# AdaLN feed-forward kernel on Trainium2: GpSimd issues three of the opening loads, and SP and ScalarE issue fourteen of the first block's sixteen squares

## The reference

```python
w = weights[conditions]                               # 128 of 200 matrices, 32x32
hidden = einsum('bct,bcd->bdt', x, w)                 # (128, 32, 256)
h = square(relu(hidden @ up_w))                       # 256 -> 1024
shared = h @ down_w                                   # 1024 -> 256
scale = top_k(hidden @ gate_w, 2)[0].sum(-1)          # 8 experts
y = shared + (hidden @ expert_weight) * scale
out = x + layernorm(y) * gamma + beta
```

## Time and profile before

| | us |
|---|---|
| median of 3 runs (229.6 to 229.78) | 229.66 |
| the profiled execution, whole | 229.29 |
| its span, first to last instruction | 227.6 |
| PE busy in the span | 220.9 |
| DVE (VectorE) busy | 160.9 |
| POOL (GpSimd) busy | 131.4 |
| ACT (ScalarE) busy | 106.4 |

### The profile page before, as it was taken

One profiled execution on the slowest core, in us unless ns is written; L12 is line 12 of the kernel. 1 busy time (PEld: TensorE's weight loads), 2 busy tenths in 40 slices (PEclk: granted clock), 3 DMA queues, 4 the chain that ended last, 5 costly groups with the idle time before them and its releaser, 6 DMA issues.

```text
span 227.6 us, 3998 instructions
## 1 busy us (share of the span) xinstructions
PE 220.9 (97%) x1260; PEld 191.4 (84%) x1260; DVE 160.9 (71%) x352; ACT 106.4 (47%) x187; POOL 131.4 (58%) x131
## 2 busy tenths in 40 slices
PE   7899999999999999999999999999999999999992
PEld 2798888888888889888889888888888888888892
DVE  6587965777667777667667766577766766777885
ACT  3379865444555345534545444544454444444000
POOL 3758795665545763656455764366555575557411
PEclk9999999999999999999999999999999999999999
DMA  3877123030603010000200002000020002000031
GB/s 98 231 213 230 50 59 103 10 98 7 187 10 98 9 66 30 0 0 3 92 0 0 3 0 95 3 0 0 0 95 1 0 0 68 28 0 0 10 108 69
DMA packets 17177, 11.81 MB, mean 52 GB/s; under 512 B 6660, under 2 KB 16900, under 8 KB 17156
## 3 DMA queue, kind: packets, MB, share of 16 engines
q1 hardware_dynamic: 15460, 10.43, 15.1%
q10 hardware_dynamic: 1280, 1.07, 1.4%
q0 software_dynamic: 416, 0.05, 0.2%
HBM read 7.35 MB, written 4.19 MB: 51 GB/s over the span
## 4 chain that ended last, share of the span: by engine, by line
PE 94%; DMA 1%; issue 1%; DVE 1%; ACTq 1%; POOLq 0%; POOL 0%; ACT 0%; DVEq 0%
PE up_ps L337 39%; PE down_ps L431 25%; PE down_ps L433 13%; PE hid_ps L303 5%; PE moe_ps L449 3%; PE moe_ps L448 3%; PE moe_ps L447 3%; DMA wd<-in_L_cond_weights_dram 1%; PE down_ps L303 1%; ACTq L513 1%; DMA cond_row<-in_itok_B_dram 1%; POOLq L46 0%; POOL rstd L697 0%; DVE result L615 0%; DVE stats L588 0%
## 5 line engine op out<-in xcount | busy, mean ns | idle before, releaser
L682 POOL TENSOR_TENSOR sq_lo<-square,sq_hi 128x512 fp32r<-128x512 f32 x64 | 84.4, 1322 | 77.0 <-DVE square L553 77.0
L431 PE MATMUL down_ps<-down_hl,sq_hi 128*128 128x512 f32 x248 | 88.8, 393 | 0.0
L553 DVE SCALAR_TENSOR_TENSOR square<-up_ps,relu 128x512 f32<-128x512 f32 x64 | 44.0, 687 | 37.3 <-ACT relu L491 28.2
L433 PE MATMUL down_ps<-down_hl,sq_lo 128*128 128x256 f32 x248 | 69.6, 280 | 0.0
L431 PEld LDWEIGHTS down_ps<-down_hl,sq_hi 128*128 128x128 f32 x248 | 46.5, 188 | 10.8 <-issue 0.3
L491 ACT ACTIVATE relu<-up_ps 128x512 f32<-128x512 f32 x64 | 38.2, 596 | 35.8 <-PE up_ps L337 35.7
L337 PE MATMUL up_ps<-hid_hi,up_hi 128*128 128x512 f32 (+1 forms) x136 | 52.8, 391 | 0.3 <-ACT hid_hi L476 0.3
L337 PE MATMUL up_ps<-hid_hi,up_lo 128*128 128x512 f32 (+1 forms) x136 | 51.1, 379 | 0.0
L433 PEld LDWEIGHTS down_ps<-down_hl,sq_lo 128*128 128x128 f32 x248 | 46.7, 188 | 2.4
L493 ACT ACTIVATE sq_hi<-relu 128x512 fp32r<-128x512 f32 x64 | 40.6, 634 | 2.0
L337 PE MATMUL up_ps<-hid_lo,up_hi 128*128 128x512 f32 (+1 forms) x136 | 40.6, 381 | 0.0
(11 more groups left out here) (62 smaller groups left out, 193.3 us busy)
## 6 DMA issues: line engine op xcount, KB each, us to landing
x_sb<-in_x_dram SPq DMA_DIRECT2D x7, 512.0 KB, 4.2
out_dram<-result SPq DMA_DIRECT2D x7, 512.0 KB, 3.0
wd<-in_L_cond_weights_dram SPq DMA_DIRECT2D x111, 4.0 KB, 1.5
x_sb<-in_L_ffn_down_w_dram SPq DMA_DIRECT2D x2, 512.0 KB, 4.7
x_sb<-in_x_dram ACTq DMA_DIRECT2D x2, 256.0 KB, 2.9
result<-in_L_ffn_up_w_dram ACTq DMA_DIRECT2D x2, 256.0 KB, 2.9
result<-in_L_ffn_up_w_dram SPq DMA_DIRECT2D x1, 512.0 KB, 4.7
out_dram<-result SPq DMA_DIRECT2D x4, 128.0 KB, 1.7
```

The costliest lines, as they stand in the source:

```text
L431: pe.matmul(dst[:, :], a_hi, down_hl[:, c, :, :].rearrange("p s t -> p (s t)"), start=(c == 0), stop=False)
L433: mm = pe.matmul(dst[:, T:2 * T], a_lo, down_hl[:, c, 0, :], start=False, stop=(c == CH - 1))
L553: dve.scalar_tensor_tensor(square[:, c % 2, :], up_ps[c % UPB][:, :], 0.0, relu[:, c % 2, :], ALU.max, ALU.mult).then_inc(square_done, 1)
L682: pool.tensor_tensor(sq_lo[:, j % 2, c, :], square[:, c % 2, :], sq_hi[:, j % 2, c, :].bitcast(f32), ALU.subtract).then_inc(sq_lo_done, 1)
```

## The change

GpSimd's list begins with three bulk loads: up's second quarter, x's second half and up's second half, ahead of its registers and squares. ScalarE's and SP's loads of these are gone. Of block 0's squares SP issues 0, 1, 4, 5 and 12 to 15, ScalarE 2, 3, 6, 7 and 8, 9 (all before `split_up(0)`), GpSimd 10 and 11, after a new wait for x's first half. Of block 1's squares SP issues six and GpSimd ten. There is now one semaphore for each group's squares and one for GpSimd's two; PE waits for group 2 and group 3 apart. VectorE rounds and splits up's second half in two parts, one before the first square, the other around the second one. Bytes and arithmetic are the same.

```diff
-UP_SPLITS = [slice(0, 2), slice(2, 4), slice(4, CH)]
+UP_LOADS = [slice(0, 2), slice(2, 4), slice(4, CH)]
+UP_SPLITS = [slice(0, 2), slice(2, 4), slice(4, 6), slice(6, CH)]
-BY_SP, BY_ACT, BY_POOL, BY_SP_LATER = (0, 2, 4, 6), (1, 3, 5, 7), (8, 9, 10, 11, 12), (13, 14, 15)
+BY_SP, BY_ACT, BY_POOL = (0, 1, 4, 5), (2, 3, 6, 7), (10, 11)
+BY_ACT_LATER, BY_SP_LATER = (8, 9), (12, 13, 14, 15)
+SECOND_BY_SP = 6
...
             for b in BY_SP_LATER:
-                sp.dma_start(square_of(b), weights_of(values[b])).then_inc(wd_later_landed[0], 16)
-            load_up(sp, 2)
+                sp.dma_start(square_of(b), weights_of(values[b])).then_inc(wd_first_landed[b // Q], 16)
...
-            second = range(TILES * Q, TILES * Q + HALF_BLOCK)
+            second = range(TILES * Q, TILES * Q + SECOND_BY_SP)
...
-                    pe.wait_ge(wd_later_landed[0], 16 * len(BY_SP_LATER))
-                    pe.wait_ge(wd_later_landed[1], 16 * len(BY_POOL))
-                    for k in range(K):
-                        condition(0, k, 2)
-                        condition(0, k, 3).then_inc(hid_done, 1)
+                    pe.wait_ge(wd_first_landed[2], 16 * len(BY_ACT_LATER))
+                    pe.wait_ge(wd_pool_landed, 16 * len(BY_POOL))
+                    condition(0, 0, 2)
+                    condition(0, 1, 2)
+                    pe.wait_ge(wd_first_landed[3], 16 * Q)
+                    condition(0, 0, 3).then_inc(hid_done, 1)
+                    condition(0, 1, 3).then_inc(hid_done, 1)
...
-            values = conditions(mybir.EngineType.Activation, range(0, HALF_BLOCK))
+            values = conditions(mybir.EngineType.Activation, range(2, 2 + HALF_BLOCK))
             act.wait_ge(wd_zeroed[0], 1)
             for b in BY_ACT:
                 act.dma_start(square_of(b), weights_of(values[b])).then_inc(wd_first_landed[b // Q], 16)
+            for b in BY_ACT_LATER:
+                act.dma_start(square_of(b), weights_of(values[b])).then_inc(wd_first_landed[b // Q], 16)
             split_up(0)
-            load_up(act, 1)
-            load_x_first(act, 1)
...
-            dve.tensor_copy(up_hi[:, :, split_cols(2)], up_raw[:, :, split_cols(2)]).then_inc(up_hi_ready, 1)
+            round_up(2)
             split_up(2)
...
+                        round_up(3)
+                    if j == 0 and c == 1:
+                        split_up(3)
...
             pool.memset(minus_half[:, :], -0.5).then_inc(consts_ready, 1)
+            load_up(pool, 1)
+            load_x_first(pool, 1)
+            load_up(pool, 2)
             pool.wait_ge(cond_first_landed, 16)
             values = conditions(mybir.EngineType.Pool, range(HALF_BLOCK, 2 * HALF_BLOCK))
             pool.wait_ge(wd_zeroed[0], 1)
+            pool.wait_ge(x_first_landed[0], 16)
             for b in BY_POOL:
-                pool.dma_start(square_of(b), weights_of(values[b])).then_inc(wd_later_landed[1], 16)
+                pool.dma_start(square_of(b), weights_of(values[b])).then_inc(wd_pool_landed, 16)
             pool.wait_ge(cond_later_landed, 16)
-            second = range(TILES * Q + HALF_BLOCK, 2 * TILES * Q)
+            second = range(TILES * Q + SECOND_BY_SP, 2 * TILES * Q)
```

More of the change, by code:

```diff
@@ L109, in adaln_ffn @@
         x_landed = {j: sem(f"x_landed{j}") for j in range(1, BLOCKS)}
-        up_landed = [sem(f"up_landed{n}") for n in range(len(UP_SPLITS))]
+        up_landed = [sem(f"up_landed{n}") for n in range(len(UP_LOADS))]
         down_landed = [sem(f"down_landed{n}") for n in range(DOWN_LOADS)]
@@ L113, in adaln_ffn @@
         cond_first_landed, cond_later_landed = map(sem, ("cond_first_landed", "cond_later_landed"))
-        wd_first_landed = [sem(f"wd_first_landed_group{g}") for g in range(TILES // 2)]
-        wd_later_landed = [sem("wd_later_landed_sp"), sem("wd_later_landed_pool")]
+        wd_first_landed = [sem(f"wd_first_landed_group{g}") for g in range(TILES)]
+        wd_pool_landed = sem("wd_first_landed_by_pool")
         wd_second_landed = [sem("wd_second_landed_sp"), sem("wd_second_landed_pool")]
@@ L220, in weights_of, with load_up @@
             return cond_w[bass.ds(row, 1), :, :].rearrange("s c d -> (s c) d")
-        def load_up(queue, part):
-            cols = split_cols(part)
-            queue.dma_start(up_raw[:, :, cols], up_rows[:, :, cols]).then_inc(up_landed[part], 16)
+        def load_up(queue, load):
+            cols = slice(P * UP_LOADS[load].start, P * UP_LOADS[load].stop)
+            queue.dma_start(up_raw[:, :, cols], up_rows[:, :, cols]).then_inc(up_landed[load], 16)
         def load_x_first(queue, half):
@@ L325, in conditioning @@
                     if j == 1:
-                        pe.wait_ge(wd_second_landed[0], 16 * HALF_BLOCK)
-                        pe.wait_ge(wd_second_landed[1], 16 * HALF_BLOCK)
+                        pe.wait_ge(wd_second_landed[0], 16 * SECOND_BY_SP)
+                        pe.wait_ge(wd_second_landed[1], 16 * (TILES * Q - SECOND_BY_SP))
                     else:
@@ L621, in split_up, with round_up @@
                                   up_hi[:, :, split_cols(part)].bitcast(f32), ALU.subtract).then_inc(up_lo_ready, 1)
+            def round_up(part):
+                dve.tensor_copy(up_hi[:, :, split_cols(part)], up_raw[:, :, split_cols(part)]).then_inc(up_hi_ready, 1)
             def split_down(part):
```

## The result

The changed kernel takes 236.19 us (median of 4 runs, 235.77 to 236.61) against 229.72: ratio 1.0289, 95% interval 1.0267 to 1.0311 (so are the intervals in brackets below). It is 6.5 us slower, where I had forecast 0.5 and a range up to 231.6.

The account below looks back on a forecast made before the run. PE, busy 97% of the span, was taken as the bound; +0.65 us for late squares and -0.15 for VectorE's split made +0.5 on the 229.66 median: 230.15 us, overall range 229.2 to 231.6.

Parts of the forecast that it names:

- the last square, issued at 4.64, lands at 4.64 + 2.6 = 7.24 (+0.60): Block 0's start: group 1's last square, PE's last real wait, lands later than today's 6.64; +0.65 us taken.
- The contention: Opening: first eight squares share the transfer engines with 1 MB more, landing in 2.6 us instead of 1.6.
- The length of the bulk: Opening: 1.5 MB at 0.38 MB/us keep the transfer engines full for 4 us, from 2.0 to 6.0 or later.
- Issue order of the first eight squares: cost nothing: Opening: SP and ScalarE still issue four each from 3.06 to 4.99, the last at 4.64; no cost.
- The clock: Rival, chance 0.06: PE's clock falls in the sparse gap before the first up product; loss 1.6 us, 231.3.
- VectorE's split, -0.15: Block 0's first square: splitting up's second half in two lets it start at 13.1; saves 0.15 us.
- The stumble at up(0, 4): PE from 14.17 to 15.02: four matmuls take 0.85 us, need 0.70, waiting for VectorE's first square; expected to go.
- GpSimd's issue price: GpSimd's three bulk loads at the start: 0.8 us each taken, possible range 0.57 to 4.5 us.
- GpSimd is not late for block 1: Block 1's squares land at 14.1 to 16.3, before PE wants them at 16.69; lateness was a rival, chance 0.16.
- SP's part costs nothing in the profile: SP's queue: one more later square, no up load, fewer second-block squares; those come about 1 us sooner, hidden.
- a late start of PE is paid at the end in full: Whole kernel: PE never waits once going, so a microsecond gained or lost before it starts is one at the end.

Follow-up runs that it names:

- experiment 7: Changed kernel with GpSimd issuing up's second half (512 KB) behind its squares 10 and 11, not ahead of them; 233.66 us, ratio 1.0171.
- experiment 1: Changed kernel with the three bulk loads back on ScalarE and SP; squares, registers and VectorE's split stay as changed; 234.29 us, ratio 1.0211.
- experiment 3: Changed kernel with ScalarE loading its registers in two steps, 0 to 7 before its first four squares, 8 and 9 behind; 235.22 us, ratio 1.0246.
- experiment 4: Changed kernel with 26 warm-up matmuls in place of 10, to keep PE busy through the wait; 233.96 us, ratio 1.0192.
- experiment 6: Kernel before the change with only VectorE's split of up's second half in two parts; 230.18 us, ratio 1.0021.
- experiment 10: Kernel before the change with GpSimd's three bulk loads ahead of all else and 26 warm-up matmuls in place of 10; 233.37 us, ratio 1.0176.
- experiment 2: Kernel before the change with only the three bulk loads moved to GpSimd, ahead of all else; 235.20 us, ratio 1.0256.

## Why the prediction was wrong

**The step that failed** is "the last square, issued at 4.64, lands at 4.64 + 2.6 = 7.24 (+0.60)". Group 1's last square is issued at 5.8 and lands 4.7 us later, at 10.5, 3.8 us late in place of 0.6: 1.1 of it is the later issue (below), the rest the time to land. Nor was it the square that PE waited for; that was group 0's, issued at 4.81 and landed at 9.68. The contention was named, its direction too; what I had was a rate of delay read off three squares (2.6 against 1.6 us) as though it were a property of a loaded stretch. Those three had under 3 us of bulk left in front of them. In the changed kernel the first eight squares, issued from 3.1 to 5.8, have 3 to 6, and take 3.3 to 4.9 to land; with less bulk or none in front they take 2.5 to 3.0 (experiment 7) or 1.4 to 1.8 (experiment 1). The earlier trace rows held the better price: GpSimd's eight squares beside SP's bulk, 4.0 to 4.6 us, the very figure that SP's showed. I read that row and took the nearer kind of transfer.

**The length of the bulk** was too short as well: 1.5 MB "from 2.0 to 6.0 or later" at 0.38 MB/us. From 4 to 6 us they move at 233 GB/s (a DMA share of 0.72, where I wanted over 0.8), and the last of them lands at 9.0. Why the rate is lower while squares and bulk go side by side wasn't tried.

**"Issue order of the first eight squares: cost nothing"** failed. I compared the number of registers and not where the load starts: 1.2 us later for ScalarE's squares, 0.9 us at the first up product (experiment 3), about 1 at the end, where the intervals overlap.

**The clock** was a rival at 0.06, priced at 1.6 us. It fell because the wait was 3.7 us and not 0.6, and it cost 2.2 (experiment 4). The price was near, and the chance depended on the term above. I had treated the two as separate cases; they are one.

**VectorE's split, -0.15,** had the wrong sign: +0.5 us (experiment 6). The stumble at up(0, 4) does go (20.57 and the next matmul are 0.23 apart). What I left out is who else waits for the first square, and that the second would be late.

**What held:** GpSimd's issue price (0.91, 0.74 and 0.72 us for the 0.8 that I took), that GpSimd is not late for block 1, though that is luck, that SP's part costs nothing in the profile, and that a late start of PE is paid at the end in full (4.26 of the 7.1 us). The luck: GpSimd's last square of block 1 is issued at 13.3 us, not at 11.9, mostly since its second register load takes 2.3 us and not 0.73, and lands at 17.4, when PE would have wanted it at 17.2 (16.69 + 0.5) by my forecast; PE comes to it only at 22.9. The loss is not that shift alone: the clock and the waits at the experts come on top. By the experiments the 6.5 us are, as an estimate: the bulk with the clock kept up, 233.37 - 229.42 = 3.95 (experiment 10, with some 0.3 of `eg_lo`'s wait in it); the clock 2.2; ScalarE's registers about 1.0; VectorE's split 0.5. These make 7.6. They probably overlap, at `eg_lo` and where a shorter wait also spares the clock, and I haven't split the 1.1 us further. Nor do they add up the other way: the change without its bulk costs 4.8 us (experiment 1), as ScalarE's own loads then come late.

Open: why a register load that starts at index 2 or 22 is three to four times slower. GpSimd's second load, of indices 22 to 31, takes 2.3 us where that of 24 to 31 took 0.6. But in both kernels one of SP's 16-index loads takes 2.0 to 2.1 us and the others 1.0, so the start alone may not be the rule.

## What to carry to other kernels

Ahead of a load that is needed soon, count the bytes already in flight at its issue, on all queues together: small transfers asked for behind a megabyte mostly took 4 to 5 us here and not 1.6, and it made no difference which queue carried the bulk. A wait that grows by microseconds must be priced together with the clock that falls in it, as one case. And before an instruction is made earlier, look at who is released by it: here a first square 0.4 us sooner let GpSimd in ahead of VectorE, and the change cost more than it gave.

## What the runs showed of the hardware that was not expected

- Squares of 4 KB took 4.4 and 4.5 us (median) behind 1 MB of bulk, in packets of 1 to 2 KB on ScalarE's queue or 4 KB on GpSimd's alike, and 1.6 us without.
- Eight registers from index 0 loaded in 0.75 us, eight from index 2 in 1.96, ten from index 22 in 2.31.
- GpSimd's issue of a load of 256 runs took 0.72 to 0.91 us against 0.50 for a square's 32.
- The granted clock was 0.50 for 3.3 us in the profiled execution of experiment 2 and for 6.7 us in the changed kernel. It differed between executions of one kernel: in experiment 2 those with a mean clock of 0.985 took 0.6 to 1.7 us longer than the one with 0.991.
- One 128x528 subtraction on VectorE took 0.70 or 1.82 us, the latter when GpSimd had started 0.04 us ahead of it.
